# Attention over pairs of units: the order on TensorE and the copies of the turned probabilities

## The reference

```python
for l in range(L):                                    # L = 2
    q = ((x @ Wq[l].T + bq[l]) * scaling).reshape(n, H, DH)   # n = 1250, H = 8, DH = 64
    k = (x @ Wk[l].T).reshape(n, H, DH)
    v = (x @ Wv[l].T).reshape(n, H, DH)
    scores = jnp.einsum('ehd,ehd->eh', q[tgt], k[srcidx])
    m = jax.ops.segment_max(scores, tgt, num_segments=n)
    p = jnp.exp(scores - m[tgt])
    s = jax.ops.segment_sum(p, tgt, num_segments=n)
    w = p / (s[tgt] + 1e-16)
    agg = jax.ops.segment_sum(w[:, :, None] * v[srcidx], tgt, num_segments=n)
    ...
```

## Time and profile before

| | us |
|---|---|
| median of three runs | 1958.04 (1957.48 to 1959.77) |
| the profiled execution's own time | 1963.22 |
| its span, first to last instruction | 1961.4 |
| TensorE matmuls busy | 1712.3 (87%) |
| VectorE busy | 1298.1 (66%) |
| ScalarE busy | 1116.6 (57%) |
| mean granted TensorE clock | 0.917 |

### The profile page before, as it was taken

The page is one execution under the profiler, slowest core; times in us unless marked ns, Lnnn a source line. Parts: engine busy times, 40 slices in busy tenths (PEclk is TensorE's granted clock), DMA queues, the critical chain, the costliest instruction groups (busy, mean ns, idle before and its releaser), DMA issues. The chain is left out here.

```text
span 1961.4 us, 35996 instructions
## 1 busy us (share of the span) xinstructions
PE 1712.3 (87%) x14256; PEld 1557.8 (79%) x14256; DVE 1298.1 (66%) x2317; ACT 1116.6 (57%) x1682; POOL 95.5 (5%) x86
## 2 busy tenths in 40 slices
PE   6995899995768999982979999997697999999777
PEld 5994899995647999982978888887696888888752
DVE  6883999992337999956326676766632667666666
ACT  2543788884215888873436777662443776776220
POOL 0000000000540000010000000002000000000300
PEclk8998999998886999995989999998898999999885
DMA  4111122212212010002672332002267133200212
GB/s 163 45 47 54 60 95 97 95 47 75 87 42 115 27 51 26 25 1 95 161 199 63 69 69 56 2 2 53 67 159 189 53 69 69 56 2 2 53 42 69
DMA packets 77097, 134.86 MB, mean 69 GB/s; under 512 B 13193, under 2 KB 52209, under 8 KB 75680
## 3 DMA queue, kind: packets, MB, share of 16 engines
q1 hardware_dynamic: 76960, 132.98, 23.6%
HBM read 89.58 MB, written 32.01 MB: 62 GB/s over the span
## 5 line engine op out<-in xcount | busy, mean ns | idle before, releaser
L1119 PE MATMUL banks<-h_gat,probs_t_gat 125*125 (+2 forms) x3200 | 377.2, 274 | 0.0
L1119 PEld LDWEIGHTS banks<-h_gat,probs_t_gat 125*125 125x125 f32 x3200 | 368.2, 191 | 0.0
L1591 ACT COPY probs_t_att<-banks 125x1250 f32<-125x1250 f32 x160 | 192.3, 1202 | 170.5 <-PE banks L1550 170.5
L1074 DVE SCALAR_TENSOR_TENSOR probs_gat<-a_src_pair_gat,a_dst_gap_gat,a_low_pair_gat 125x1250 f32<-125x1250 f32 x160 | 240.6, 1505 | 24.4 <-DMA a_low_pair_gat<-a_src_rows 24.4
L1111 PE MATMUL banks<-ident,probs_gat 125*125 125x125 f32 x1600 | 213.3, 282 | 49.6 <-ACT probs_gat L1041 49.6
L1618 DVE CUSTOM_DVE_ANT_0 probs_att<-banks,logs_or_y 125x1250 f32<-125x1250 f32 x160 | 233.5, 1460 | 29.9 <-PE banks L1541 29.9
L1111 PEld LDWEIGHTS banks<-ident,probs_gat 125*125 125x125 f32 x1600 | 194.8, 195 | 51.1 <-ACT probs_gat L1041 51.1
L1079 DVE CUSTOM_DVE_ANT_0 probs_gat<-probs_gat,log_counts 125x1250 f32<-125x1250 f32 x160 | 233.7, 1461 | 0.0
L1041 ACT ACTIVATE probs_gat<-probs_gat,neg_max_gat 125x1250 f32<-125x1250 f32 x160 | 212.9, 1331 | 33.4 <-DVE neg_max_gat L1079 32.9
L1584 ACT ACTIVATE probs_att<-probs_att,neg_max_att 125x1250 f32<-125x1250 f32 x160 | 214.9, 1343 | 11.0 <-DVE neg_max_att L1618 10.9
L1562 PE MATMUL banks<-probs_t_att,v_rows 125*64 125x125 f32 x3200 | 206.5, 275 | 0.1
(11 more groups left out here) (214 smaller groups left out, 2651.7 us busy)
## 6 DMA issues: line engine op xcount, KB each, us to landing
logs_or_y<-log_rows SPq DMA_DIRECT2D x20, 610.4 KB
q_first<-q_rows SPq DMA_DIRECT2D x12, 1000.0 KB
q_rows<-q_out_qkv SPq DMA_DIRECT2D x40, 250.0 KB
a_src_pair_gat<-a_src_rows SPq DMA_DIRECT2D x16, 610.4 KB
a_low_pair_gat<-a_src_rows SPq DMA_DIRECT2D x16, 610.4 KB
q_att<-q_rows SPq DMA_DIRECT2D x8, 1000.0 KB
log_counts<-counts_fr SPq DMA_DIRECT2D x50, 122.1 KB
gat_rows<-final_gat SPq DMA_DIRECT2D x16, 312.5 KB
```

What stands on the lines that cost most here:

```text
L1074: dve.scalar_tensor_tensor(probs[:, n.tile % B], a_src[:, n.parity], a_dst_gap[:, n.tile, bass.ds(n.head, 1)], a_low[:, n.parity], ALU.add ...
L1119: total = pe.matmul(out_bank(n.tile), probs_t[:, n.tile % B, i], h_sb[:, i, bass.ds(n.head * CH, CH)], start=i == 0, stop=i == T - 1)
L1591: act.copy(probs_t[:, u % TURNED].rearrange("p (b c) n -> p b (c n)", c=2), turned).then_inc(probs_saved, 1)
```

## The change

In `stage_attend` alone:

- The PSUM buffer of the turn is no longer five half banks but three banks, with 4, 3 and 3 transposes (`CUTS`), 500, 375 and 375 columns. ScalarE copies each bank by an instruction of its own, and each bank has its own step in the semaphores (`piece_turned`, `piece_saved`): turn u waits, bank by bank, for the copies of turn u-1.
- TensorE's order goes by pairs. For pair p: turn 2p, turn 2p+1, score 2p+4, the whole weighing of pair p-1, score 2p+5. The first pair's turns stand between scores 2, 3, 4 and 5.
- ScalarE: the copies of both turns, exponentials 2p+3 and 2p+4, the output copy of pair p-1 (a pair earlier than before).
- VectorE: mask u+1, safe u, divide u.

```diff
-    HALF = BANK // 2
+    CUTS = ((0, 4), (4, 7), (7, 10))
+    PIECES = len(CUTS)
...
-        turned = k.psum[0:P, 3 * BANK:3 * BANK + T // 2 * HALF].rearrange("p (b c) -> p b c", c=HALF)[:, :, 0:W]
+
+        def turned(j):
+            lo, hi = CUTS[j]
+            return k.psum[0:P, (3 + j) * BANK:(3 + j) * BANK + (hi - lo) * P]
...
             def turn(u):
                 pe.wait_ge(divided, u + 1)
-                if u >= 1:
-                    pe.wait_ge(probs_saved, u)
+                for j, (lo, hi) in enumerate(CUTS):
+                    if u >= 1:
+                        pe.wait_ge(piece_saved, (u - 1) * PIECES + j + 1)
+                    for i in range(lo, hi):
+                        block_t = pe.transpose(turned(j)[:, (i - lo) * P:(i - lo + 1) * P],
+                                               probs[:, u % SLOTS, i * P:(i + 1) * P], k.ident[0:P, 0:P])
+                    block_t.then_inc(piece_turned, 1)
+
+            def weigh(p):
+                pe.wait_ge(piece_saved, (2 * p + 2) * PIECES)
+                if p >= 2:
+                    pe.wait_ge(att_saved, p - 1)
                 for i in range(T):
...
-            for u in range(UNITS):
-                turn(u)
-                if u >= 2:
-                    weigh(u // 2 - 1, u % 2)
-                if u + 3 < UNITS:
-                    score(u + 3)
-            for part in range(2):
-                weigh(PAIRS - 1, part)
+            turn(0)
+            score(3)
+            turn(1)
+            score(4)
+            score(5)
+            for p in range(1, PAIRS):
+                turn(2 * p)
+                turn(2 * p + 1)
+                if 2 * p + 4 < UNITS:
+                    score(2 * p + 4)
+                weigh(p - 1)
+                if 2 * p + 5 < UNITS:
+                    score(2 * p + 5)
+            weigh(PAIRS - 1)
...
             def save_turned(u):
-                act.wait_ge(probs_turned, u + 1)
                 if u >= TURNED:
                     act.wait_ge(summed, (u - TURNED) // 2 + 1)
-                act.copy(probs_t[:, u % TURNED].rearrange("p (b c) n -> p b (c n)", c=2), turned).then_inc(probs_saved, 1)
+                for j, (lo, hi) in enumerate(CUTS):
+                    act.wait_ge(piece_turned, u * PIECES + j + 1)
+                    act.copy(probs_t[:, u % TURNED, lo:hi].rearrange("p c n -> p (c n)"), turned(j)).then_inc(piece_saved, 1)
...
-            for u in range(UNITS):
-                save_turned(u)
-                if u + 2 < UNITS:
-                    exponential(u + 2)
-                if u % 2 == 0 and u >= 4:
-                    save_att(u // 2 - 2)
-            for p in range(PAIRS - 2, PAIRS):
-                save_att(p)
+            save_turned(0)
+            exponential(2)
+            save_turned(1)
+            exponential(3)
+            exponential(4)
+            for p in range(1, PAIRS):
+                for u in (2 * p, 2 * p + 1):
+                    save_turned(u)
+                for u in (2 * p + 3, 2 * p + 4):
+                    if u < UNITS:
+                        exponential(u)
+                save_att(p - 1)
+            save_att(PAIRS - 1)
...
-            for u in range(2):
-                mask(u)
-            safe(0)
-            divide(0)
+            mask(0)
             for u in range(UNITS):
                 if u + 1 < UNITS:
-                    safe(u + 1)
-                if u + 2 < UNITS:
-                    mask(u + 2)
-                if u + 1 < UNITS:
-                    divide(u + 1)
+                    mask(u + 1)
+                safe(u)
+                divide(u)
```

## The result

The changed kernel takes 1964.93 us (median of 11 runs), the kernel before 1958.04 (11 runs): ratio 1.0034, 95% interval 1.0023 to 1.0046. It is **slower by 0.34%** where 1950.8 and faster was forecast. The time lies inside the range; the sign is wrong.

What follows compares the result with a forecast made beforehand. TensorE's instruction stream was taken as the bound. A pair: 6.96 plus stall 0.27 = 7.23 against 7.32; with start and end -3.6 a layer, -7.2 for two, from 1958.0 to 1950.8. Range 1934 to 1967.

Steps and rivals of the forecast that it cites:

- What bounds the kernel: Attention stage: TensorE's own instruction stream sets the pace; ScalarE and VectorE have about 1 us slack per 3.66 us unit.
- (1): TensorE, weighing: one whole weighing per pair instead of two halves saves one round trip, 0.36 us a pair.
- The new seams: TensorE: turn to score no hole; score to weighing taken as 0.10 in the pair's slots, from a range of 0 to 0.17.
- (2): TensorE, odd turn: its first load waits for ScalarE's copy of the first bank, stall 0.27 a pair, bounds 0.17 to 0.57.
- Rival B: Second turn of every pair: copies don't overlap or each waiting load costs a restart; 1962 to 1973, chance 0.18.
- forecast's own signs of being wrong: TensorE: odd turn over 1.6 us, holes between turn and score, or the clock rows falling.
- (3): ScalarE: three copies instead of one, 1.21 against 1.10 a unit; slack 1.0, costed at nothing.
- (4): VectorE: order mask, safe, divide; reciprocal 0.1 longer a unit, slack 0.6 before the score, costed at nothing.
- (5): SyncE: loads of q and the log counts wait for scores and masks as before; costs nothing.
- (6): Start of the layer: score 4 starts 1.1 earlier, score 5 waits for mask 4, turn 2 at 1041.05.
- (7): End of the layer: from turn 76 the sum is 11.93; the waits of the last units go.
- Clock: TensorE clock stays at 1.00; the rival, that it falls while 20 transposes and a stall stand together: 2004, chance 0.04.

Runs made afterwards that it cites:

- the run with wide weights: Four-bank kernel with weighing weights 128 columns wide, 20 matmul records instead of 40, the odd unit's sum left out: 1916.85 us in one execution, pair 6.73.
- the repaired kernel: Changed kernel with the order of two waits swapped, ahead of a turn's first transpose and ahead of the first copy: 1951.25 us, ratio 0.9962.
- the four-bank one: Changed kernel with the turn's three pieces going around four banks, the fourth taken from the two output banks: 1932.82 us, ratio 0.9860.

## Why the prediction was wrong

Point by point, by the steps of the prediction:

- **What bounds the kernel**: right. TensorE's stream sets the pace; what was put into or taken out of a pair (7.32, 7.37, 7.25, 6.98, 8.12, 7.77) reached the time, as far as the spread of the runs can tell.
- **(1) One round trip less, 0.36**: right; 0.34 measured without a stall. The new seams were as taken: no hole between turn and score, and 0.10 between score and weighing (it starts 0.19 after the score's last matmul, where the next one otherwise follows after 0.10). Two turns and the score behind them take 3.42 without a stall, where the sum had 3.44. The whole weighing takes 2.30, 0.03 over the 2.27 of the sum; the sum's own figures, 20 x 0.1065 + 0.07 + 0.09, make 2.29. That its weights are the cause was an inference; the run with wide weights bears it out except for the question left open there.
- **(2) The stall: the step that failed.** 0.27 was forecast, 0.39 measured. The mechanism was right and also the form of the wait: one a pair, at the first bank of the odd turn, none at the others. The size was off in two terms: "a copy starts 0.31 after the start of its last transpose" was 0.36, and the load, which "0.05 later" was to go, went 0.11 after the copy's end. Both figures came from places where the late wait is the one on the instruction itself: the copy of before, whose source waits for the turn first and the weighing second, and a load of the weighing. The diff exchanges the two waits ahead of the copy, and ahead of the turn the copy's wait already stood second, where it had rarely been late. So in the changed kernel both late waits are taken by a semaphore instruction of their own, and the copy or the load has still to start afterwards. The sum priced neither. With the waits exchanged the terms of the chain come out as predicted.

The price stood in the trace of before, at the very turn from which the restart of 0.21 was taken. That turn, too, waits for the copy ahead of it:

```profile
1033.71 1.21 ACT L1591 COPY probs_t_att<-banks 125x1250 f32<-125x1250 f32 x1 [3.21 <-PE banks L1550]
...
1035.03 1.17 PEld L1550 LDWEIGHTS banks<-ident,probs_att 125*125 125x125 f32 x10 [0.26 <-issue]
```

The copy ends at 1033.71 + 1.21 = 1034.92 and the turn's load goes at 1035.03: 0.11, with "issue" in the bracket, as in the changed kernel. With this row in place of the weighing's the stall would have been put at 0.33, and with the copy's 0.05 as well at 0.38.

- **How close the repaired kernel came** is in part luck. 1951.25 against 1950.8 are medians beside different runs of the kernel before; from the first score to the last weighing, both layers together, it saves 606.0 - 600.6 = 5.4 us where the sum had 7.2.
- Rival B named the point: "it decides from a stall of 0.36 on". The stall was 0.39, and a slower kernel had 0.23 of the chances. But its mechanism (copies that don't overlap, late second and third pieces) isn't what happened: copies overlap, pieces 2 and 3 were in time (copies end 1.64 and 2.02 after the pair's start, their banks are wanted from 1.81 and 2.14). None of the forecast's own signs of being wrong came either: the odd turn lasts 1.42, turn and score stand without a hole, the clock holds through the stretches. They were set for other mechanisms.
- **(3), (4), (5)** nothing: right. ScalarE has its slack in spite of 11 us more work in a stretch of 263 us, and the old order of VectorE shows what step (4) avoided.
- **(6) start**: turn 2 was put 19.98 after the first score (1041.05 - 1021.07); it came after 19.98 in the first layer and 19.69 in the second. The hit in the first is luck: score 5 started 0.7 earlier than forecast and was 0.7 longer at the lower clock. **(7) end**: 11.93 forecast, 12.25 in the second layer (1800.32 to 1812.57); with the waits exchanged 12.01, so 0.24 of the 0.32 is the two stalls.
- **Clock**: 1.00 in both stretches of 263 us, also with 20 transposes in a row. At the start of the first layer it fell to 0.50 once, as told above; in no other profile here does it fall within the attention. The rule of the Trainium skill ("TensorE: Matmul & The Clock Gate", "Part 4: PE-mode transpose") would have had the clock at risk; the stretches of the changed kernel and of the four-bank one, with 20 transposes in a row in every pair, don't bear that out.

The sum in one line: -0.34 for the round trip, +0.39 for the stall. The forecast's gain of 0.09 was what was left of a gain of 0.36 and a loss of 0.27, and the loss was 0.12 too small.

## What to carry to other kernels

When two passes over one buffer are put side by side, price the whole chain between them: the last write, the wait of the copier, the copy, the wait of the next writer, the restart. Where one of these instructions has two waits, find out which one comes last in the run and put that wait first in the code; here that was worth 0.7% and the sign. A forecast whose gain is the difference of two large terms should carry the error of both; and if the stall can't be shortened, look for a buffer that is held without need: one of two output banks was, and using it made the kernel 1.4% faster than the one before.

## What the runs showed of the hardware

- Of two waits ahead of one instruction, the one written last in the source became a semaphore instruction of its own (kernel before, changed kernel and the one with the waits exchanged, on TensorE and ScalarE).
- If the late wait is the separate one, the instruction starts later: a copy on ScalarE 0.36 instead of 0.31 after the start of the last transpose, a load on TensorE 0.11 instead of 0.05 after the end of the copy. With four banks, where no turn waits for a copy, the exchange is worth nothing that the times show (6.98 and 6.97 a pair).
- One way into and out of the paired matmuls with 64 weight columns costs TensorE 0.34 us at full clock; with 128 columns and no pairs the pair of units is 0.25 shorter.
- A copy from PSUM took 0.575 for 125 x 500 and 0.48 to 0.49 for 125 x 375, close to the line through 1250 and 125 columns (0.57 and 0.465), and the next copy starts 0.10 to 0.12 before it ends.
